# A DLRM tower on one core: a third of the label slabs multiplied whole on VectorE, summed on ScalarE

## What is computed

```python
q1, q2 = attn_pool(x, w1, b1, w2), attn_pool(x, w3, b3, w4)
h = concatenate([q1, q2], axis=1) @ w5 + b5
f6 = h @ w6 + b6
cross = h[:, iu] * h[:, ju] * g            # all pairs i < j of 300
f7 = cross @ w7 + b7
out8 = concatenate([f6, f7], axis=1) @ w8 + b8
z = einsum('bu,bku->bk', out8, label_embedding)   # 1024 x 200, from 1024 x 200 x 300
h = relu(concatenate([z, dense_ctx], axis=1) @ W_top1 + b_top1)
y = relu(h @ W_top2 + b_top2) @ W_top3
```

## Time and profile before

| | |
|---|---|
| median of 3 runs (lowest to highest) | 1843.5 us (1841.83 to 1844.25) |
| span of the profiled execution, first to last instruction | 1839.3 us |
| its own time outside that span | not shown; the median is 4.2 us above the span |
| PE busy | 1686.2 us, 92% |
| DVE busy | 1666.4 us, 91% |
| ACT busy | 1028.9 us, 56% |
| POOL busy | 556.3 us, 30% |
| moved by DMA | 561.70 MB, mean 305 GB/s |

### The profile page before, as it was taken

One profiled execution on the slowest core, in us unless ns is written; L12 is line 12 of the kernel. 1 busy time (PEld: TensorE's weight loads), 2 busy tenths in 40 slices (PEclk: granted clock), 3 DMA queues, 4 the chain that ended last, 5 costly groups with the idle time before them and its releaser, 6 DMA issues.

```text
span 1839.3 us, 26080 instructions
## 1 busy us (share of the span) xinstructions
PE 1686.2 (92%) x7084; PEld 1247.3 (68%) x7084; DVE 1666.4 (91%) x5850; ACT 1028.9 (56%) x3233; POOL 556.3 (30%) x413
## 2 busy tenths in 40 slices
PE   2888999999999999999999999999998999997751
PEld 1555667777777777777777777777776777765531
DVE  5999979989999889999999999999999888777776
ACT  3786684674466644465654764456653544464534
POOL 7777508727300226400087028400000000000053
PEclk9889999999999999999999999999999999999975
DMA  9489856848978698989769776997749999989975
GB/s 279 115 282 323 287 167 219 330 158 304 376 301 309 228 358 328 367 329 346 294 206 351 272 257 208 403 419 277 256 155 407 421 407 381 392 320 419 421 302 240
DMA packets 97054, 561.70 MB, mean 305 GB/s; under 512 B 15567, under 2 KB 15941, under 8 KB 71309
## 3 DMA queue, kind: packets, MB, share of 16 engines
q1 hardware_dynamic: 77629, 498.39, 70.5%
q0 software_dynamic: 19264, 61.64, 10.6%
q10 hardware_dynamic: 16, 0.00, 0.0%
HBM read 559.98 MB, written 0.00 MB: 304 GB/s over the span
## 4 chain that ended last, share of the span: by engine, by line
PE 60%; DVE 21%; DMA 8%; POOL 5%; issue 4%; ACT 2%; SPq 0%; DVEq 0%; ACTq 0%; POOLq 0%
PE acc L1010 53%; DVE junk L628 10%; DMA w_sb<-in_w 7%; DVE qa L670 6%; DVE prod L780 5%; POOL x L571 3%; PE coarse L859 2%; POOL lab L571 2%; DMA lab<-in_labels 1%; PE acc L925 1%; PE misc L932 1%; ACT waste L1130 1%; PE acc L891 1%; PE acc L906 1%; PE acc L909 1%
## 5 line engine op out<-in xcount | busy, mean ns | idle before, releaser
L1010 PE MATMUL acc<-w_sb,prod 128*128 128x300 f32 (+2 forms) x5648 | 1522.1, 420 | 50.9 <-DMA w_sb<-in_w 32.7
L1010 PEld LDWEIGHTS acc<-w_sb,prod 128*128 128x128 f32 (+2 forms) x5648 | 1040.6, 191 | 394.8 <-DMA w_sb<-in_w 43.9
L1235 ACT ACTIVATE prod<-prod,g_all 128x256 f32<-128x256 f32 (+4 forms) x1615 | 685.9, 469 | 465.2 <-DVE prod L780 462.8
L571 POOL DMA_INDIRECT x<-in_tbl,ids_sb x368 | 479.2, 1302 | 652.2 <-DVE qa L670 546.2
L780 DVE TENSOR_TENSOR prod<-fine,coarse 128x1280 f32<-128x1280 f32 (+4 forms) x325 | 424.6, 1312 | 97.4 <-PE coarse L859 93.7
L628 DVE SCALAR_TENSOR_TENSOR junk<-lab,heads 128x300 bf16<-128x300 f32 x1208 | 478.1, 464 | 7.2 <-DMA lab<-in_labels 7.1
L628 DVE SCALAR_TENSOR_TENSOR junk<-x,heads 128x300 bf16<-128x300 f32 x1128 | 445.4, 463 | 21.7 <-DMA x<-in_tbl,ids_sb 21.6
L670 DVE SCALAR_TENSOR_TENSOR qa<-x,ex,qa 128x300 f32<-128x300 f32 x612 | 276.1, 532 | 0.0
L602 POOL TENSOR_TENSOR x<-x,out 128x2400 f32<-128x2400 f32 x5 | 26.2, 5254 | 597.2 <-ACT out L1105 588.7
L1130 ACT ACTIVATE waste<-x 128x300 bf16<-128x300 f32 x368 | 161.5, 439 | 24.5 <-DMA x<-in_tbl,ids_sb 24.3
L1054 ACT ACTIVATE picked<-hh 128x256 f32<-128x256 f32 (+4 forms) x325 | 121.5, 374 | 0.0
(11 more groups left out here) (107 smaller groups left out, 520.9 us busy)
## 6 DMA issues: line engine op xcount, KB each, us to landing
w_sb<-in_w SPq DMA_DIRECT2D x320, 750.0 KB, 6.7
lab<-in_labels SPq DMA_DIRECT2D x146, 1200.0 KB, 8.9
x<-in_labels SPq DMA_DIRECT2D x54, 1200.0 KB, 11.2
x<-in_tbl,ids_sb POOLq DMA_INDIRECT x368, 5.7
w_sb<-in_w SPq DMA_DIRECT2D x5, 450.0 KB, 5.9
prod<-in_v_i SPq DMA_DIRECT2D x1, 710.0 KB, 4.3
prod<-in_v_j SPq DMA_DIRECT2D x1, 710.0 KB, 7.4
w_sb<-in_w SPq DMA_DIRECT2D x1, 703.1 KB
```

What stands on the lines that cost most here:

```text
L571: pool.indirect_dma_start(out=row_of(t, n), out_offset=None, in_=tables[n], in_offset=bass.IndirectOffsetOnAxis(ap=ids_sb[:, t, n:n + 1], ...
L1010: last = pe.matmul(acc[:, t % 3, 0:EMB], prod[0:rows, u % RING, m, t % 2 * P:(t % 2 + 1) * P], w7_sb[0:rows, u % W7_RING, m * EMB:(m + 1) ...
L1235: act.activation(chunk, chunk, ACT.Copy, scale=g_all[0:rows, pair:pair + 1]).then_inc(chunk_ready, 1)
```

## The change

Of tiles 0 to 5, the slabs with `s % 3 == 1` (1, 4, ..., 22: eight of a tile, 48 in all, listed in `BY_ACT`) are no longer done as 8 rows. DVE multiplies the whole slab, 2400 elements of each partition, in one instruction, in place, with `row8` repeated 8 times by a step of zero. ACT then sums each of the 8 rows with an activation that gives its sum into `z`; these 8 instructions are put on eight ticks in a row, one per tick, from the first tick of the next unit. Two semaphores are added. SP's load into such a slab's place waits for the ACT sums, and so does PE's transpose of `z`. In `plan()` such a slab costs 5 less, and its place is held 114 (two units) longer; `slot_free` reads these new ends. The rest of the kernel's text is the same, but all three orders come out of `plan()` again.

```diff
--- before.py
+++ after.py
@@ -78,6 +78,8 @@
 CHAIN0 = 16
 
 
+BY_ACT = [t * SLABS + s for t in range(TILES) for s in range(SLABS) if s % 3 == 1 and t < 6]
+
 def active(u):
 
     return sorted((t for t in range(TILES) if STARTS[t] <= u < ENDS[t]), key=lambda t: t % 2)
@@ -162,6 +164,7 @@
 
 
     before, items, tail = [], [[] for _ in range(TOTAL)], []
+    slot_end, sum_tick = [], 0
     pool_ticks, loads = {}, [(0, "w7", u) for u in range(W7_RING)]
     dots = [("dots", t, h) for t in range(1, TILES) for h in range(HALVES)]
     rest = [item for t in range(1, TILES) for item in
@@ -180,8 +183,8 @@
         if switch is not None and n >= switch:
             if n < switch + X_SLOTS:
                 return weighed[TILES - 1, HALVES - 1]
-            return slab_end[n - END_SLOTS]
-        return slab_end[n - SLOTS] if n >= SLOTS else weighed.get((1, HALVES - 1), 1e9)
+            return slot_end[n - END_SLOTS]
+        return slot_end[n - SLOTS] if n >= SLOTS else weighed.get((1, HALVES - 1), 1e9)
 
     while c < TOTAL or len(slab_end) < len(slabs):
         u, nslab, due, held = c - 1, len(slab_end), 1e9, False
@@ -236,6 +239,13 @@
         kind, t, h = item
         now += COST[kind]
         if kind == "slab":
+            slot_end.append(now)
+            if len(slab_end) in BY_ACT:
+                now -= 5
+                for k in range(SLAB):
+                    sum_tick = max(sum_tick + 1, (u + 1) * FINE)
+                    pool_ticks.setdefault(sum_tick, []).append(("sum", len(slab_end), k))
+                slot_end[-1] = now + 2 * UNIT[2]
             slab_end.append(now)
             continue
         if kind == "dots":
@@ -286,7 +296,12 @@
 ROWS_BEFORE, _rows = {}, JUNK
 for _item in [("dots", 0, h) for h in range(HALVES)] + BEFORE + [i for u in ITEMS for i in u] + TAIL:
     ROWS_BEFORE[_item] = _rows
-    _rows += ROWS_OF.get(_item[0], 0)
+    _rows += ROWS_OF.get(_item[0], 0) if _item[0] != "slab" or _item[1] * SLABS + _item[2] not in BY_ACT else 0
+
+
+def sums_before(n):
+
+    return SLAB * sum(m < n for m in BY_ACT)
 
 
 def slab_slot(n):
@@ -463,6 +478,8 @@
         slab_loaded = [sem(f"slab_loaded{i}") for i in range(END_SLOTS)]
         y_stored = sem("y_stored")
         multiplied = sem("multiplied")
+        products_ready = sem("products_ready")
+        products_summed = sem("products_summed")
         sums_done = sem("sums_done")
         copy_ready = sem("copy_ready")
         context_ready = sem("context_ready")
@@ -555,6 +572,8 @@
                     held = n - SLOTS if n < SWITCH else n - END_SLOTS
                     if held in BY_POOL:
                         sp.wait_ge(sums_done, SLAB * (BY_POOL.index(held) + 1))
+                    elif held in BY_ACT:
+                        sp.wait_ge(products_summed, sums_before(held + 1))
                     else:
                         sp.wait_ge(rows_done, ROWS_BEFORE["slab", held // SLABS, held % SLABS] + SLAB)
                 sp.dma_start(slab_place(slot).rearrange("p k e -> p (k e)"),
@@ -797,6 +816,12 @@
                     dve.wait_ge(copy_ready, t + 1)
                 slot, loads = slab_slot(t * SLABS + s)
                 dve.wait_ge(slab_loaded[slot], 16 * loads)
+                if t * SLABS + s in BY_ACT:
+                    rows = slab_place(slot).rearrange("p k (h e) -> p k h e", h=2)
+                    times = bass.AP(tensor=row8.tensor, offset=row8.offset,
+                                    ap=[list(row8.ap[0]), [0, SLAB], list(row8.ap[1]), list(row8.ap[2])])
+                    dve.tensor_tensor(rows, rows, times, ALU.mult).then_inc(products_ready, 1)
+                    return
                 for k in range(SLAB):
                     row(ROWS_BEFORE["slab", t, s] + k, slab_place(slot)[:, k, :], row8,
                         z[:, t % Z_RING, s * SLAB + k:s * SLAB + k + 1], 2)
@@ -912,6 +937,7 @@
 
             def turn_z(t):
                 pe.wait_ge(rows_done, ROWS_BEFORE["slab", t, SLABS - 1] + SLAB)
+                pe.wait_ge(products_summed, sums_before((t + 1) * SLABS))
                 pe.wait_ge(context_ready, t + 1)
                 if t == TILES - 1:
                     pe.wait_ge(sums_done, SLAB * len(BY_POOL))
@@ -1139,6 +1165,15 @@
                     product = slab_place(slot)[:, k, :]
                     act.activation(product, product, ACT.Copy,
                                    accum_out=z[:, (TILES - 1) % Z_RING, column:column + 1]).then_inc(sums_done, 1)
+
+            def sum_product(n, k):
+
+                act.wait_ge(products_ready, BY_ACT.index(n) + 1)
+                slot, _ = slab_slot(n)
+                t, s = divmod(n, SLABS)
+                product = slab_place(slot)[:, k, :]
+                act.activation(product, product, ACT.Copy,
+                               accum_out=z[:, t % Z_RING, s * SLAB + k:s * SLAB + k + 1]).then_inc(products_summed, 1)
 
             def exp_scores(t, fields=range(FIELDS)):
                 act.wait_ge(rows_done, ROWS_BEFORE["dots", t, fields[-1] // FG] + HALF)
@@ -1246,6 +1281,8 @@
                             exp_scores(t)
                         elif name == "exp_softmax":
                             exp_softmax(t)
+                        elif name == "sum":
+                            sum_product(t, i)
             respond("f7s", TILES - 1, 0, 0)
             for name, of, n in END_BURSTS:
                 if name == "zt":
```

## The result

The changed kernel is slower: a median of 1866.53 us (1862.25 to 1868.42, 4 runs) against 1842.66 us of the kernel before (1839.64 to 1844.25, 4 runs), a ratio of 1.0131, with a 95% interval from 1.0114 to 1.0147. The forecast was 1832.6 us, 0.6% faster, and its range ended at 1845. The profiled execution took 1862.25 us, its span is 1860.5, 21.2 more than before. An execution here takes 1.75 us longer than its own span, so the 4.2 us of the kernel before compare two executions; the forecast is the same with either.

What follows compares the result with a forecast made beforehand. PE, busy 92% of the span, was taken to bound the kernel, losing time to DVE and `w7` loads in three stretches, with the last 30 units going by bytes. Six terms summed to -10.9 us, giving 1832.6 us, range 1825 to 1845.

Steps and rivals of the forecast that it cites:

- Term 3: Units 246 to 252: slab 111's load sorts later, one slab less stands before `w7` 250; -2.9 us, bounds 0 and -9.7.
- Term 4: The end: two slab loads fewer before the last `w7` loads, so PE ends earlier; -5.9 us, bounds 0 and -5.9.
- Term 1: Units 90 to 110: DVE is late and whole-slab multiplication relieves it; -3.2 us, bounds 0 and -3.6.
- Term 2: Units 167 to 175: PE is behind DVE, and four tile 2 slabs get cheaper; -1.9 us, bounds 0 to -2.5.
- Term 6: Places held for the sums: DVE stalls about 1 us where it takes one slab per unit; +1.5 us, bounds 0 and 10.
- Prices of instructions: DVE's whole-slab instruction 2.66 us, saving 25 us over 48 slabs; ACT's 384 sums 0.44 us each, 169 us more.
- Term 5: Sums and absolute sums on the same tick, some 41 ticks, mostly hidden on ACT; +1.5 us, 18 if nothing hid it.
- SP's queue standing at the sums: Rival: SP waits in order for ACT's sums, holding up `w7` loads behind; +21, 1853.6 us, chance 0.12.
- ACT doesn't pace as that rival had it: Rival that ACT paces: accumulator read not overlapped, a sum costs 0.62 us; +12, 1844.6 us, chance 0.04.
- The order doesn't pay at the end: Rival: late slabs are made up by late loads, the end comes as before; 1840.5 us, about no change, chance 0.20.
- if DVE's idle time behind slab loads goes from 7 us to tens with PE waiting for chunks: One of the signs named in advance that would show the prediction wrong.

Runs made afterwards that it cites:

- experiment 2: The changed kernel with only the 5 taken off the plan's cost undone, the place still held 114 longer; 1846.86 us, 1.0029 against the kernel before.
- experiment 3: The changed kernel's order, but every slab done by rows, with no sums on ACT and no place held for them; 1866.03 us, 1.0129.
- experiment 4: The changed kernel without ACT's 384 sums; a slab's place is free when DVE has multiplied it; 1855.08 us, 1.0072.
- experiment 7: The changed kernel with only the plan's time from a free place to a landed slab raised from 45 to 90; 1841.32 us, 0.9997.
- experiment 9: Control: the kernel before with only the plan's time from a free place to a landed slab raised from 45 to 90; 1836.29 us, 0.9962.
- experiment 6: The changed kernel with the 5 undone and the plan's time from a free place to a landed slab raised from 45 to 90; 1827.57 us, 0.9924.
- experiment 8: The changed kernel with the 5 undone and whole-slab multiplication only in tiles 0 and 2, 16 slabs; 1838.32 us, 0.9983.
- experiment 10: The changed kernel with 90 for 45 as the plan's slab landing time and without ACT's 384 sums; 1834.48 us, 0.9954.
- experiment 12: The changed kernel, 5 undone, landing time 90 for 45, slab 107 by rows, slab 111 planned 64 later; 1833.54 us, 0.9951.
- experiment 5: The kernel before with slab 111 counted ready 109 later in the plan, no whole-slab multiplications or sums; 1837.87 us, 0.9978.
- experiment 1: The changed kernel with the order of the kernel before: neither the 5 nor the longer hold in the plan; 1976.0 us, 1.0739.
- experiment 11: The changed kernel, 5 undone, landing time 90 for 45, slab 111 planned 100 later still; 1830.2 us, 0.9933.

## Why the prediction was wrong

**The step that failed** is the premise of terms 3 and 4, of slab 111 that "its load sorts at 13223" and "two slab loads fewer stand in front of the last `w7` loads". They were worked out with the hold alone, on the order of the kernel before; the 5 were taken only as a cheaper item. But `plan()` puts items into a unit until its clock reaches the time at which the next `cross` is due. With 5 less, one more item fits into some units (87, 89, 93, 97, 101), and slabs creep three to six ahead of the old order: 91 and not 87 are done by unit 210, 101 and not 98 by 220, 111 and not 105 by 240, `SWITCH` moves from 112 to 116, and before the last `w7` there are 183 loads where the forecast had 180. By `plan()` without the hold the 5 alone make almost the same order (92 by unit 210, 111 by 240). In the order that the forecast had in hand (experiment 2) the gains of terms 1, 2 and 4 are there, and the loss is 0.3% instead of 1.3%. The changed kernel has one slab of tile 6 in `TAIL`, where the forecast had one or two more than the two of before.

**Term 6 was mis-sized**, in both orders. It said "DVE stalls about 1 us at such slabs" from a load of 8.9 us and a slab per unit at even spacing, +1.5 us, at most 10. Measured are 28.5 us of stalls after and 42.4 in experiment 2. It counted when a place comes free and how long a median load takes, and left out two things. The held place's load goes out behind those of one or two later slabs, and where the DMA moves 400 GB/s at a share of 1.01 those bytes have to pass first (experiments 3 and 4: out 18 and 19 us before its use, slab 89 stalls DVE all the same). And the plan takes a slab 4.5 us after its load's time, while the load takes 13.4 us at slab 89. The median load told nothing of this: it is shorter after (7.8 us) than before. Experiment 7 against the change puts the price of the 45 at 25 us, experiment 9 against the kernel before at 7, so some 18 to 25 us are the change's. In the order with the hold alone (experiment 2 against 6) it is 19, or 12 with the same 7 taken off. A run with the place held and the slab loads kept in their own order wasn't made, so how the price divides between the late place in the queue and the 4.5 us is not shown.

Term by term:

- **Prices of instructions**: right (2645 ns, 439 ns, DVE 26 us less busy, ACT 166 more). Eight rows take 3.12 us, not 3.10, from start to start. On the new one the formula that the prediction took from the Trainium skill, page "VectorE: DVE Perf Modes", its errata section, gives 2.66 us; the trace agrees within 1%.
- **Term 1** (-3.2): right in experiments 2, 6 and 8 (-3.4 to -3.5), and nothing of it after, with or without sums (129.5 and, in experiment 10, 129.3). By the orders, units 87, 89, 93, 97 and 101 have an item more and others one less, and PE is slower than before in units 87, 88, 93, 98 and 101 and faster in others; DVE's saving goes where PE doesn't wait. That wasn't run alone. From the start of unit 90 to that of unit 110 after takes 112.9 us against 113.4, not the 110 announced:

```profile
507.97 5.22 PE L1036 MATMUL acc<-w_sb,prod 128*128 128x300 f32 x20
...
620.90 5.21 PE L1036 MATMUL acc<-w_sb,prod 126*128 126x300 f32 x20
```

- **Term 2** (-1.9): right in its own stretch, units 167 to 175: 43.7 us before, 42.1 after, 41.9 and 41.3 in experiments 2 and 6. In the wider stretch from 163 to 180 it is -3.6 and -4.2 there, and +0.2 after, which has the stall of slab 73 in it and some 2 us of sums (experiments 7 and 10).
- **Term 3** (-2.9): experiment 12 gives -2.0. The late place of slab 111 that brings it also brings DVE's longest stall, 17.8 and 16.5 us in experiments 2 and 6. After, the stretch gains 5.4, but the stretches beside it lose more (+3.9 and +3.1). `SWITCH` is at 116 there and the crowd of loads lies otherwise; no run isolates this.
- **Term 4** (-5.9): the mechanism is right, -4.8 in experiment 5 and -5.8 in experiment 6. After, +2.5. The bound stretch moves its bytes as before, so it is the count of slab loads that tells. The windows of the end (after, columns as in the earlier trace rows):

```profile
1660.00:1777.00 117.00, 91.18 (x351) 61.62 (x349) 89.58 (x368) 57.74 (x204) 0.00 (x0) 0.97 1.01 420
1777.00:1795.00 18.00, 7.36 (x30) 4.81 (x30) 7.25 (x11) 3.48 (x13) 7.03 (x2) 0.89 0.28 116
```

  420 GB/s as in the earlier trace rows, and 116 in the lull: the loads that should have moved into it stand ahead of it. The forecast weighed 358 GB/s a core from the Trainium skill, "DMA: Bandwidth & Descriptors", § Bandwidth. The same section gives about that figure for two cores that stream at once and 425 GB/s for a 16 MB transfer of one core alone; this kernel runs on one core, and its stretches of 418 to 420 GB/s agree with the latter.
- **Term 5** (+1.5, bounds 0 and 18): 6.8 us without stalls (experiment 10), 11 with them. The places that the sums hold are in both prices. The forecast looked only at ticks with a sum and an absolute sum, and took nearly all as hidden; by experiments 7 and 10 PE loses 0.9 to 2.5 us in each of four stretches. Term 5 is too small by 5 to 6 us.

**The rivals.** SP's queue standing at the sums is a real mechanism (experiment 1), but not what happened. ACT doesn't pace as that rival had it: a sum is 439 ns as in the earlier trace rows, its read overlapped. Experiment 3 is as slow without any, but it lacks DVE's saving too; against experiment 4 the sums do cost 11 us of the 24. "The order doesn't pay at the end" is right of the end and too mild elsewhere. What did happen, loads planned too close to their use, stood in the prediction's last sentence as a sign of failure, "if DVE's idle time behind slab loads goes from 7 us to tens with PE waiting for chunks", and had no chance or price of its own beyond term 6. Slab loads that overtake each other stood nowhere.

**What adds up**, by the ratios: after stands 1.0131 - 0.9997 = 0.0134 above experiment 7, 25 us; 7 us of such a step show before too (experiment 9), so 18 are put down to the change's own late loads. That the 7 may be taken off is an argument and not shown: 2.8 of them lie in units 296 to 324, behind one slab load less (181 and not 182), a gain that experiment 7 hasn't, so up to 25 may be the change's own. The sums are 7 to 8 (experiment 10). Experiment 10 stands 0.9954 - 0.9962 = -0.0008 from experiment 9, so the order with the 5 and all that DVE saves bring 1.5 us together, which is within the noise. 18 + 8 - 1.5 is some 24 us. These are steps from one run to the next, so they close by themselves: the sum says how the loss divides and is no check of it. The gains of terms 1 to 4 are real and need the order without the 5: experiment 6.

**What stays open**: why experiment 2's stall of 17.8 us at slab 111 cost PE some 5 to 7 us (45.7 us for units 247 to 252, against 40.3 before and 38.2 in experiment 6) where the 16.5 us in experiment 6 cost none. In experiment 2 PE waits 12.3 us in one piece for a chunk there, in experiment 6 it waits 4.4 us for `w7` and 0.5 for chunks. `LOADS` is the same there in both. But DVE takes slab 111 among the items of unit 249 in experiment 2 and of unit 250 in experiment 6, one `cross` later, so PE has a unit more of chunks before it when the stall begins. That is the likely reason; it wasn't run alone.

## What to carry to other kernels

Where an order is made by a planner, a changed cost is a changed order: run the planner and count again whatever the argument rests on (here the loads ahead of the last `w7`), cost by cost, before pricing anything by the old order. Whoever holds a buffer longer must look at the latency the plan grants its reload, and at which later loads now go out ahead of it: the 4.5 us planned cost 0.4% before, 1.1% once the plan held places 11.4 us longer, and 1.3% in the order with the 5. And a control with the repair alone tells how much of a gain is the change's: of experiment 6's 0.76%, half came with the repair (0.38% in experiment 9).

## What the runs showed that was not expected

In one and the same kernel a label load of 1200 KB took 5.3 us from issue to landing at slab 98 and 13.4 at slab 89, while the median is 7.8. The difference is what else the DMA moves: 293 GB/s at a share of 0.83 around slab 98, 402 GB/s at 1.02 around slab 89. And in a full queue the order counts more than the time of issue: in experiment 4 the same load went out 6.3 us earlier relative to DVE and the stall was 0.6 us shorter. Last, idle time of DVE is worth nothing or nearly everything by what PE waits for at the moment: 16.5 us cost none in experiment 6 (experiment 11, without them, is no faster), 9.9 us cost 8.8 in units 210 and 211 of the changed kernel.
